# Mixture-of-experts stage: two of four gate/up products as float32r pieces, x copied by ScalarE, gate weight read through the owner's register, loop lap starting with the transposes

## The chip, the cores and the metric

The kernel runs on one core of one Trainium2 chip. The time is device microseconds of one execution; a smaller time is better. The kernel before takes 1219.33 us (median of 3 runs, 1219.15 to 1221.19).

## The reference

The reference is one decoder block on 2048 rows of width 512: a state-space mixer, a cross attention and a mixture of experts, each behind a layer norm and added to its input. The change touches only the last part:

```python
router_logits = (x @ gate_w).astype(jnp.float32)
scores = jax.nn.sigmoid(router_logits)
_, selected = jax.lax.top_k(scores + expert_bias[None, :], K)        # K = 2 of E = 16
top_scores = jnp.take_along_axis(scores, selected, axis=1)
top_scores = top_scores / (top_scores.sum(-1, keepdims=True) + 1e-20)
shared = jax.nn.silu(x @ shared_gate_w) * (x @ shared_up_w) @ shared_down_w
comb = jnp.zeros((T, E), jnp.float32).at[jnp.arange(T)[:, None], selected].add(top_scores)
routed = jnp.zeros_like(x)
for e in range(E):
    gu = x @ experts_gate_up[e]                                      # 512 -> 2 x 256
    g, u = jnp.split(gu, 2, axis=-1)
    routed = routed + comb[:, e:e + 1] * (jax.nn.silu(g) * u @ experts_down[e])
return (shared + routed).reshape(b, s, h)
```

## The kernel before

The mixer and the attention run first (the first 900 us of the span); nothing there is changed. `experts_phase` then sorts the 4096 (row, expert) pairs into 47 tiles of 128 rows, each tile owned by one expert, and works through the tiles, numbered n = 0 to 46. Each of TensorE (PE), VectorE (DVE), ScalarE (ACT), GpSimd (POOL) and the DMA queue of SyncE (SP) has its own program; they meet only at semaphores, and each engine runs its program in the written order.

For a tile n the work is:

- POOL gathers the 128 rows into one of six buffers `xg` (L1512). A row carries its 512 values and behind them its 16 gate weights.
- PE turns them (`transpose_x`, four 128x128 transposes, L1879, semaphore `tx`), and DVE copies the result from PSUM to `xgT` (L1588, `txc`). `xgT` has two buffers.
- PE multiplies by the owner's gate/up weights (`gate_up`, L1909, semaphore `gu`): four float32 products over k. The profile lists each float32 product as two matmuls, so eight matmuls a tile. The weights are read from `ring`, at a slot that is read into a register from the table `own_i`.
- ACT takes the silu of the first half (L1750, `sg`), DVE multiplies by the second half (L1694, `h`), PE turns `h` (`transpose_h`, L1918, `th`); this stands in the middle of the next tile's `gate_up`.
- The product with the down weights is made of float32r pieces: a number is split as high + low, where high is its float32r copy. ACT writes the high pieces (`down_high` from `ring`, L1757; `hT_high`, L1762), DVE the low ones (`down_low`, L1706; `hT_low`, L1712), and PE does high*high, high*low and low*high, six float32r matmuls a tile (`down`, L1927 to L1929, semaphore `dn`).
- ACT scales the result by the row's gate weight `share` (L1771), and POOL adds it into `out` with two indirect DMAs (L1523). `share` is made by DVE: 16 gates times a one-hot `mask`, then a sum (L1699, L1700).

In the steady state PE's order is: `gate_up(n)` with `transpose_h(n-1)` in its middle, `transpose_x(n+1)`, `down(n-1)`. The programs of ACT and DVE are written out for all 47 tiles, and each loads the ring slot of a tile from `own_i` (one value) once per tile, ahead of its read of `ring` (L1428). PE's program is a loop of 7 laps with six tiles each (L1952), with three tiles ahead of it and two behind. At the start of a lap PE loads 12 values (six owners, six slots) into registers with one instruction (L1888). ACT, DVE and PE each have a sequencer, which carries out the register loads and the waits in program order and hands the other instructions to the engine; its own instructions stand in the profile's rows under PEldq, ACTq and DVEq. Expert weights come through a ring of four slots, filled by SP.

Of the kernel before, what the change touches and what calls it, by code (L numbers as in the profile page):

```python
# [11 lines left out]
F32R = mybir.dt.float32r  # L12
# [4 lines left out]
P = 128  # L17
# [1291 lines left out]
def experts_phase(nc, dram, x1, score, ident, out, kept):  # L1309
# [8 lines left out]
    E = 16  # L1318
# [12 lines left out]
    CUTS = 6  # L1331
    HALF = mybir.dt.float16
    ROW = D + E
    xn_rows = dram["xn_rows"]

    with ExitStack() as ctx:
# [38 lines left out]
        source = sb("source", [P, T, TOP, TILES], HALF)  # L1375
        place = sb("place", [P, PAIRS, P], HALF)
        listed = sb("listed", [P, TOP, TILES])
# [4 lines left out]
        mask = sb("mask", [P, TILES, E])  # L1382
        share = sb("share", [P, TILES])
        shares = sb("shares", [P, E])
        logit = sb("logit", [P, P])
# [9 lines left out]
        xg = sb("xg", [P, XG, ROW])  # L1395
        xgT = sb("xgT", [P, 2, KD * P])
        sg = sb("sg", [P, 2, F])
# [22 lines left out]
                 "xTc", "logits", "score", "route_a", "route_mm", "table", "slots", "scattered", "su", "ss", "sh",  # L1420
                 "sd", "sacc", *(f"xg{i}" for i in range(XG)), "tx", "txc", "gu", "sg", "h", "th", "thigh", "tlow", "whigh", "wlow", "dn", "yc",
# [4 lines left out]
        def slot_of(engine, n):  # L1426

            _, (place_of,) = nc.values_load_multi_w_load_instructions(  # L1428
                own_i[0:1, n, 1:2], max_val=RING - 1, min_val=0, engines=[engine],
                skip_runtime_bounds_check_because="the table holds it masked with RING - 1")  # L1430
            return place_of

        def down_weights(place_of):

            return ring[:, bass.ds(place_of, 1), WUP:WUP + KF * D].rearrange("p o c -> p (o c)")

        @block.sync
# [117 lines left out]
        def _(dve):  # L1555
# [28 lines left out]

            def copy_x(n, p):

                dve.wait_ge(s["tx"], n + 1)
                nc.vector.tensor_copy(xgT[:, p, :], ps_x[p][:, :]).then_inc(s["txc"], 1)  # L1588

# [90 lines left out]
            for j in DOWN[0:2]:  # L1680
                add_shared(j)
            copy_x(0, 0)
            for j in DOWN[2:4]:
# [3 lines left out]
                                           op0=ALU.add, op1=ALU.add).then_inc(s["dest"], 1)  # L1687
            V.then(nc.vector.tensor_tensor(mask[:, :, :], iota_e[:, :, :].to_broadcast(jwide),
                                           owner[:, :, :].to_broadcast(jwide), ALU.is_equal))

# [4 lines left out]

            def weigh(n):

                at_least(dve, s["share"], n)
                V.then(nc.vector.tensor_tensor(shares[:, :], xg[:, n % XG, D:ROW], mask[:, n, :], ALU.mult))  # L1699
                nc.vector.tensor_reduce(share[:, n:n + 1], shares[:, :], AX.X, ALU.add).then_inc(s["share"], 1)  # L1700

            def low_weights(n):

                slot_n = slot_of(mybir.EngineType.DVE, n)
                dve.wait_ge(s["whigh"], n + 1)
                nc.vector.tensor_tensor(down_low[:, :], down_weights(slot_n), down_high[:, :], ALU.subtract  # L1706
                                        ).then_inc(s["wlow"], 1)
# [7 lines left out]
            weigh(0)  # L1715
            for n in range(TILES):
                if n + 1 < TILES:
                    copy_x(n + 1, (n + 1) % 2)
                gated(n, n % 2)
                if n + 1 < TILES:  # L1720
                    weigh(n + 1)
                low_weights(n)
                low_h(n, n % 2)

        @block.scalar
        def _(act):
# [25 lines left out]
            def high_weights(n):  # L1752

                slot_n = slot_of(mybir.EngineType.Activation, n)
                act.wait_ge(s["gu"], n + 1)
                at_least(act, s["dn"], n)
                nc.scalar.activation(down_high[:, :], down_weights(slot_n), ACT.Copy).then_inc(s["whigh"], 1)  # L1757

            def high_h(n, p):
                act.wait_ge(s["th"], n + 1)  # L1760
                at_least(act, s["dn"], n)
                nc.scalar.activation(hT_high[:, :], ps_h[p][:, 0:KF * P], ACT.Copy).then_inc(s["thigh"], 1)  # L1762

            def copy_y(n, p):
# [6 lines left out]
                nc.scalar.activation(y[:, n % YB, :], ps_y[p][:, :], ACT.Copy, scale=share[:, n:n + 1]).then_inc(s["yc"], 1)  # L1771

            silu(0, 0)
            act.wait_ge(s["table"], 1)
            high_weights(0)
            for n in range(1, TILES):
                high_h(n - 1, (n - 1) % 2)
                silu(n, n % 2)
                high_weights(n)
                copy_y(n - 1, (n - 1) % 2)  # L1780
# [4 lines left out]
        def _(pe):  # L1785
# [111 lines left out]
            def gate_up(n, p, own, between=None, second=None):  # L1897

                pe.wait_ge(s["wready"], own[0])
                pe.wait_ge(s["txc"], n + 1)  # L1900
                at_least(pe, s["h"], n - 1)
                if isinstance(n, int) and n == 1:
                    pe.wait_ge(s["sacc"], 4)
                for k in range(KD):
                    if between is not None and k == KD // 2:
                        transpose_h(*between)
                    if second is not None and k == KD // 2:
                        transpose_x(*second)
                    ins = nc.tensor.matmul(ps_gu[p][:, :], xgT[:, p, k * P:(k + 1) * P],  # L1909
                                           weights(own)[:, k * 2 * F:(k + 1) * 2 * F],  # L1910
                                           start=(k == 0), stop=(k == KD - 1))
# [27 lines left out]
            def bodies(n, count, first, lap=0, last=False):  # L1939

                own = owners(n, count)
                for m in range(count):
                    more, q = divmod(first + m + 1, XG)
                    body(n + m, (m + 1) % 2, own[m],
                         after=None if last and m == count - 1 else (q, lap + more))

            transpose_x(0, 0, 0, 0)
            pe.wait_ge(s["table"], 1)
            pe.wait_ge(s["sacc"], 1)
            gate_up(0, 0, owners(0, 1)[0], second=(1, 1, 1, 0))  # L1950
            bodies(1, 2, 1)
            with pe.Fori(0, (TILES - 5) // STEP) as i:  # L1952
                bodies(STEP * i + 3, STEP, 3, i)
            bodies(TILES - 2, 2, (TILES - 2) % XG, (TILES - 2) // XG, last=True)
            transpose_h(TILES - 1, 0)
# [95 lines left out]
```

## Time and profile before

| | |
|---|---|
| median of the runs | 1219.33 us |
| the profiled execution, its own time | 1220.97 us |
| its span (first to last instruction) | 1218.0 us |
| PE matmul busy | 1159.5 us (95%) |
| DVE busy | 766.5 us (63%) |
| ACT busy | 519.6 us (43%) |
| POOL busy | 387.6 us (32%) |
| mean granted TensorE clock | 0.994 |
| the tiles of the experts | about 935 to 1212 us |

The busy shares are means over the whole span, and only the last quarter of it is changed, so what counts is the rows of that quarter. Matmuls overlap in the records: one that starts every 0.23 us is listed as 0.39 us long. The distance from start to start is the time that it takes of the engine. A time is given from the start of the span.

### The profile page before, as it was taken

The numbers are of one execution on the slowest core, as the hardware profiler recorded it, in microseconds if no ns is written. First come the engines' busy times: TensorE is split into PE (matmuls) and PEld (weight loads), VectorE is DVE, ScalarE is ACT, GpSimd is POOL, SyncE is SP. The second block draws the span as 40 slices with busy tenths as digits, with TensorE's granted clock in tenths as the row PEclk, the third lists the DMA queues.
The fourth block names the chain that finished last, engine by engine and source line by source line (L and its number), as shares of the span: only waits on it lengthen the run. The fifth ranks groups of instructions, "written<-read, shape, count | busy, mean of one in ns | idle before, by whom it ended". The sixth has DMA issues, their size and how long they took to land. (4 is left out here: it accounts for less than half of the span.)

```text
span 1218.0 us, 31770 instructions
## 1 busy us (share of the span) xinstructions
PE 1159.5 (95%) x13279; PEld 600.5 (49%) x13280; DVE 766.5 (63%) x1244; ACT 519.6 (43%) x716; POOL 387.6 (32%) x502
## 2 busy tenths in 40 slices
PE   6999999999999999999999999999999999999997
PEld 3444434444545544544545554444444555555554
DVE  3743596756788665668575787877657444455443
ACT  3321223533554453545453455555632434444443
POOL 5212311221221230132032221110102477777775
PEclk9999999999999999999999999999999999999998
DMA  8330785104284210355500246300135676788640
GB/s 196 103 88 22 186 174 112 36 16 119 60 158 96 65 33 20 84 123 107 106 25 16 68 100 93 87 3 3 72 105 171 171 181 117 163 231 234 176 89 5
DMA packets 119605, 122.26 MB, mean 100 GB/s; under 512 B 25472, under 2 KB 84992, under 8 KB 119344
## 3 DMA queue, kind: packets, MB, share of 16 engines
q1 hardware_dynamic: 101744, 98.59, 31.7%
q0 software_dynamic: 17008, 21.16, 9.4%
q8 instruction: 99, 1.62, 0.6%
q10 hardware_dynamic: 720, 0.61, 0.2%
q14 instruction: 34, 0.28, 0.1%
HBM read 94.63 MB, written 40.77 MB: 111 GB/s over the span
## 5 line engine op out<-in xcount | busy, mean ns | idle before, releaser
L684 DVE TENSOR_REDUCE mx<-ps_m 128x2 f32<-128x1024 f32 x256 | 312.9, 1222 | 192.8 <-PE ps_m L1025 188.7
L893 ACT ACTIVATE prob<-ps_s 128x1024 f32<-128x1024 f32 x256 | 261.9, 1023 | 322.7 <-PE ps_s L1025 321.8
L1025 PE MATMUL acc<-xnT,wring 128*32 128x512 f32 x1888 | 249.0, 592 | 0.6 <-DVE first_z L620 0.6
L1909 PE MATMUL ps_gu<-ring,xgT 128*128 x376 | 178.7, 598 | 12.0 <-issue 11.1
L1523 POOL DMA_INDIRECT out<-y,dest x92 | 144.7, 1573 | 76.9 <-ACT y L1771 57.7
L1025 PE MATMUL ps_s<-q_stack,k_stack 99*32 99x512 bf16 x2048 | 161.7, 380 | 4.4 <-ACT prob L893 3.8
L1025 PE MATMUL ps_m<-k_stack,q_stack 96*32 96x512 bf16 x1952 | 153.2, 380 | 9.8 <-DVE mx L684 8.2
L1210 PE MATMUL ps_o<-prob,values 128*32 128x128 f32 x4096 | 138.4, 273 | 0.0
L1210 PEld LDWEIGHTS ps_o<-prob,values 128*32 128x32 f32 x4096 | 116.3, 110 | 44.7 <-issue 39.2
L1025 PEld LDWEIGHTS ps_m<-k_stack,q_stack 96*32 96x32 bf16 x1952 | 55.7, 96 | 127.3 <-issue 72.8
L1706 DVE TENSOR_TENSOR down_low<-ring,down_high 128x1024 fp32r<-128x1024 f32 x47 | 57.6, 1226 | 67.1 <-ACT down_high L1757 67.1
L1909 PEld LDWEIGHTS ps_gu<-ring,xgT 128*128 128x128 f32 x376 | 67.3, 191 | 64.0 <-issue 61.0
L1025 PEld LDWEIGHTS ps_s<-q_stack,k_stack 99*32 99x32 bf16 x2048 | 59.0, 96 | 77.6 <-issue 41.5
L1023 PE MATMUL acc<-xnT,wring 128*128 128x512 f32 x184 | 85.6, 603 | 2.1 <-DVE xz L602 2.0
L1025 PEld LDWEIGHTS acc<-xnT,wring 128*32 128x32 f32 x1888 | 65.8, 109 | 43.1 <-issue 6.1
L1757 ACT ACTIVATE down_high<-ring 128x1024 fp32r x47 | 49.6, 1056 | 72.9 <-PE acc L1929 72.6
L1025 PE MATMUL acc<-wring,xz 128*32 128x512 f32 x576 | 76.5, 593 | 0.0
L430 POOL TENSOR_SCALAR mneg<-mx 128x16 f32<-128x16 f32 x32 | 10.1, 317 | 195.7 <-DVE mx L684 195.7
L1588 DVE COPY xgT<-ps_x 128x512 f32<-128x512 f32 x47 | 32.5, 692 | 55.2 <-PE ps_x L1879 55.2
L602 DVE SCALAR_TENSOR_TENSOR xz<-acc,convw,xz 128x511 f32<-128x511 f32 (+2 forms) x84 | 62.7, 746 | 3.9 <-ACT xz L974 1.9
L1512 POOL DMA_INDIRECT xg<-xn_rows,token x47 | 48.4, 1031 | 27.9 <-DVE token L1666 13.9
L1023 PEld LDWEIGHTS acc<-xnT,wring 128*128 128x128 f32 x184 | 34.4, 193 | 41.9 <-issue 32.7
(289 smaller groups left out, 1369.0 us busy)
## 6 DMA issues: line engine op xcount, KB each, us to landing
ring<-in_w_experts SPq DMA_DIRECT2D x96, 256.0 KB, 5.1
wring<-in_w_in SPq DMA_DIRECT2D x80, 256.0 KB, 4.3
q_stack<-part_rows SPq DMA_DIRECT2D x96, 128.0 KB, 4.7
wring<-in_w_out SPq DMA_DIRECT2D x32, 256.0 KB, 2.9
part_rows<-part SPq DMA_DIRECT2D x20, 384.0 KB, 3.8
out<-x SPq DMA_DIRECT2D x4, 1024.0 KB, 4.8
xt<-in_x SPq DMA_DIRECT2D x14, 256.0 KB, 4.6
k_stack<-part_rows SPq DMA_DIRECT2D x48, 64.0 KB, 4.1
```

The costliest lines, as they stand in the source:

```text
L602: ins = nc.vector.scalar_tensor_tensor(out=xz[:, i, tap:], in0=bank(b, 5 + i)[:, :SEQ - tap], scalar=convw[:, i, 3 - tap:4 - tap], in1=xz[ ...
L684: nc.vector.tensor_reduce(mx[:, n % G, 2 * u:2 * u + 2], ps_m[:, :, :], AX.X, ALU.max).then_inc(s_max, 1)
L893: nc.scalar.activation(prob[:, slot % PROB, :, :], ps_s[:, :, :], ACT.Exp, scale=SCALE).then_inc(s_exp, 1)
L1023: return nc.tensor.matmul(dst, stationary, moving, start=start, stop=stop)
L1025: ins = nc.tensor.matmul(dst[c:c + 32, :], stationary[:, c:c + 32], moving, start=start, stop=stop, tile_position=(0, c))
L1210: ins = nc.tensor.matmul(out_rows.rearrange("p (t i) -> p t i", i=VW), values[:, t, g, :], weights[:, a, :, :], start=(t == 0 and r == 0), ...
L1512: pool.indirect_dma_start(out=xg[:, n % XG, :], out_offset=None, in_=xn_rows[:, :], in_offset=bass.IndirectOffsetOnAxis(ap=token[:, n:n + ...
L1523: pool.indirect_dma_start(out=out[:, :], out_offset=bass.IndirectOffsetOnAxis(ap=dest[:, k, n:n + 1], axis=0), in_=y[:, n % YB, :], in_off ...
L1588: nc.vector.tensor_copy(xgT[:, p, :], ps_x[p][:, :]).then_inc(s["txc"], 1)
L1706: nc.vector.tensor_tensor(down_low[:, :], down_weights(slot_n), down_high[:, :], ALU.subtract).then_inc(s["wlow"], 1)
L1757: nc.scalar.activation(down_high[:, :], down_weights(slot_n), ACT.Copy).then_inc(s["whigh"], 1)
L1909: ins = nc.tensor.matmul(ps_gu[p][:, :], xgT[:, p, k * P:(k + 1) * P], weights(own)[:, k * 2 * F:(k + 1) * 2 * F], start=(k == 0), stop=(k ...
```

## The change

1. `gate_up` does the first two of its four products in float32 as before (`WHOLE` = 256 columns of x) and the last two (`SPLIT_K` = 2) from pieces, as `down` does: six float32r matmuls, with `transpose_h` between the two groups. The new pieces are `xgT_high` and `up_high` (written by ACT) and `xgT_low` and `up_low` (written by DVE), with the semaphores `xhigh`, `uhigh`, `xlow`, `ulow`. Each has one buffer. `up_high` and `up_low` lie where `place` was.
2. x is copied out of PSUM by ACT, in two instructions of 256 columns (`high_x`), no longer by DVE in one of 512. `xgT` now has one buffer.
3. `share` is one column read through a register that holds the owner, so `mask` and the two small DVE instructions go. ACT and DVE now load two values (owner and slot) a tile. On ACT the load stands between the silu of a tile and the copy of the next tile's x.
4. In PE's loop a step is now `transpose_x(n+1)`, `down(n-1)`, `gate_up(n+1)` with `transpose_h(n)` in it, so that a lap begins with transposes, and ends with the six float32r matmuls of `gate_up`.

```diff
+    SPLIT_K = 2
+    WHOLE = (KD - SPLIT_K) * P
...
+        def owner_of(engine, n):
+
+            _, (own, place_of) = nc.values_load_multi_w_load_instructions(
+                own_i[0:1, n, :], max_val=E, min_val=0, engines=[engine],
...
+            def low_x(n, p):
+
+                dve.wait_ge(s["xhigh"], n + 1)
+                nc.vector.tensor_tensor(xgT_low[:, :], ps_x[p][:, WHOLE:D], xgT_high[:, :], ALU.subtract
+                                        ).then_inc(s["xlow"], 1)
...
+            def weigh(n, own):
+
+                nc.vector.tensor_copy(share[:, n:n + 1], xg[:, n % XG, D - 1:ROW][:, bass.ds(own, 1)]).then_inc(s["share"], 1)
...
+            def low_up(n, place_of):
+
+                dve.wait_ge(s["uhigh"], n + 1)
+                nc.vector.tensor_tensor(up_low, up_weights(place_of), up_high, ALU.subtract).then_inc(s["ulow"], 1)
...
             for n in range(TILES):
-                if n + 1 < TILES:
-                    copy_x(n + 1, (n + 1) % 2)
                 gated(n, n % 2)
                 if n + 1 < TILES:
-                    weigh(n + 1)
-                low_weights(n)
+                    low_x(n + 1, (n + 1) % 2)
+                    own_next, slot_next = owner_of(mybir.EngineType.DVE, n + 1)
+                    weigh(n + 1, own_next)
+                    low_up(n + 1, slot_next)
+                if n:
+                    low_weights(n, slot_n)
                 low_h(n, n % 2)
...
+            def high_x(n, p):
+
+                act.wait_ge(s["tx"], n + 1)
+                nc.scalar.activation(xgT[:, :], ps_x[p][:, 0:WHOLE], ACT.Copy).then_inc(s["txc"], 1)
+                nc.scalar.activation(xgT_high[:, :], ps_x[p][:, WHOLE:D], ACT.Copy).then_inc(s["xhigh"], 1)
+
+            def high_up(n, place_of):
+
+                at_least(act, s["gu"], n)
+                nc.scalar.activation(up_high, up_weights(place_of), ACT.Copy).then_inc(s["uhigh"], 1)
...
             for n in range(1, TILES):
+                slot_n = slot_next
                 high_h(n - 1, (n - 1) % 2)
                 silu(n, n % 2)
-                high_weights(n)
+                if n + 1 < TILES:
+                    _, slot_next = owner_of(mybir.EngineType.Activation, n + 1)
+                    high_x(n + 1, (n + 1) % 2)
+                    high_up(n + 1, slot_next)
+                high_weights(n, slot_n)
                 copy_y(n - 1, (n - 1) % 2)
...
-                for k in range(KD):
...
+                for k in range(KD - SPLIT_K):
+                    nc.tensor.matmul(ps_gu[p][:, :], xgT[:, k * P:(k + 1) * P],
+                                     weights(own)[:, k * 2 * F:(k + 1) * 2 * F], start=(k == 0), stop=False)
+                if between is not None:
+                    transpose_h(*between)
+                pe.wait_ge(s["xlow"], n + 1)
+                pe.wait_ge(s["ulow"], n + 1)
+                for k in range(SPLIT_K):
+                    rows, cols = slice(k * P, (k + 1) * P), slice(k * 2 * F, (k + 1) * 2 * F)
+                    nc.tensor.matmul(ps_gu[p][:, :], xgT_high[:, rows], up_high[:, cols], start=False, stop=False)
+                    nc.tensor.matmul(ps_gu[p][:, :], xgT_high[:, rows], up_low[:, cols], start=False, stop=False)
+                    ins = nc.tensor.matmul(ps_gu[p][:, :], xgT_low[:, rows], up_high[:, cols], start=False,
+                                           stop=(k == SPLIT_K - 1))
                 ins.then_inc(s["gu"], 1)
...
-            def body(n, p, own, after=None):
-                gate_up(n, p, own, between=(n - 1, 1 - p))
-                if after is not None:
-                    transpose_x(n + 1, 1 - p, *after)
+            def step(n, p, own, q, lap):
+
+                pe.wait_ge(s["wready"], own[0])
+                transpose_x(n + 1, 1 - p, q, lap)
                 down(n - 1, 1 - p)
+                gate_up(n + 1, 1 - p, own, between=(n, p))
```

On ACT, in the written-out part for the tiles, one tile of the kernel before reads as follows (`sg` is the silu, TENSOR_LOAD the load from the table, ISA the register arithmetic ahead of an instruction with an address from a register):

```order
L1750 ACTIVATE sg<-ps_gu 128x256
L1428 TENSOR_LOAD own_i
L1757 ISA
L1757 ACTIVATE down_high<-ring 128x1024
L1771 ACTIVATE y<-acc,share 128x512
L1762 ACTIVATE hT_high<-ps_h 128x256
```

One tile of the changed kernel, on ACT at the same place:

```order
L1773 ACTIVATE sg<-ps_gu 128x256
L1432 TENSOR_LOAD own_i
L1783 ACTIVATE xgT<-ps_x 128x256
L1784 ACTIVATE xgT_high<-ps_x 128x256
L1789 ISA
L1789 ACTIVATE up_pieces<-ring 128x1024
L1778 ISA
L1778 ACTIVATE down_high<-ring 128x1024
L1803 ACTIVATE y<-acc,share 128x512
L1794 ACTIVATE hT_high<-ps_h 128x256
```

Three instructions are new, and all three stand between the load and the copy of the down weights.

On PE, the start of a lap in the kernel before (the last matmuls of `down` ahead of the branch, then the lap's load and the first matmuls of `gate_up`):

```order
L1927 MATMUL acc<-down_high,hT_high 128x512
L1928 MATMUL acc<-down_low,hT_high 128x512
L1929 MATMUL acc<-down_high,hT_low 128x512
L1952 UNCONDITIONAL_BRANCH
L1952 ISA
L1888 TENSOR_LOAD own_i
L1900 REGISTER_ALU
L30 REGISTER_ALU
L1909 ISA
L1909 MATMUL ps_gu<-ring,xgT 128x512
```

And in the changed kernel, from the last matmuls of `gate_up` on:

```order
L1956 MATMUL ps_gu<-up_pieces,xgT_high 128x512
L1957 MATMUL ps_gu<-up_pieces,xgT_high 128x512
L1958 MATMUL ps_gu<-up_pieces,xgT_low 128x512
L2005 UNCONDITIONAL_BRANCH
L2005 ISA
L1932 TENSOR_LOAD own_i
L1920 ISA
L30 REGISTER_ALU
L1923 MATMUL ps_x<-ident,xg 128x128 x4
```

The load of the 12 values still stands right behind the branch; what stands ahead of it is now the part of `gate_up` that waits for `ulow`, and what stands behind it is the transposes of x.

## Rows read from the trace of the kernel before

**Rows 1.** Waits from 937 to 1210 us: who waited, for what, total, times, longest

```profile
PE ps_gu L1909 <- issue: 11.1, 7, 1.9
```

**Rows 2.** Timeline of one tile: start, length, engine, line, instruction, idle before it

```profile
1045.24 0.60 PE L1879 MATMUL ps_x<-ident,xg 128*128 128x128 f32 x4
...
1045.44 0.38 ACT L1750 ACTIVATE sg<-ps_gu 128x256 f32<-128x256 f32 x1 [1.33 <-PE ps_gu L1909]
...
1045.88 0.69 DVE L1588 COPY xgT<-ps_x 128x512 f32<-128x512 f32 x1 [1.17 <-PE ps_x L1879]
...
1047.06 1.88 PE L1909 MATMUL ps_gu<-ring,xgT 128*128 x4
...
1047.41 1.06 ACT L1757 ACTIVATE down_high<-ring 128x1024 fp32r x1 [1.58 <-PE acc L1929]
...
1048.37 0.67 ACT L1771 ACTIVATE y<-acc,share 128x512 f32<-128x512 f32 x1
...
1048.62 1.23 DVE L1706 TENSOR_TENSOR down_low<-ring,down_high 128x1024 fp32r<-128x1024 f32 x1 [1.43 <-ACT down_high L1757]
1048.77 0.38 PE L1918 MATMUL ps_h<-ident,h 128*128 128x128 f32 x2
...
1048.99 1.88 PE L1909 MATMUL ps_gu<-ring,xgT 128*128 x4
...
1050.71 0.60 PE L1879 MATMUL ps_x<-ident,xg 128*128 128x128 f32 x4
```

**Rows 3.** Instructions of L1888, PE's load from the table: prologue, one lap, behind the loop

```profile
L1888 PEldq TENSOR_LOAD <-own_i x2: 730/870/1011, 935.3 to 937.4; - x2
...
L1888 PEldq TENSOR_LOAD <-own_i x1: 2972/2972/2972, 1056.3 to 1056.3; - x1
...
L1888 PEldq TENSOR_LOAD <-own_i x1: 1006/1006/1006, 1194.1 to 1194.1; - x1
```

**Rows 4.** Instructions of L1428, one value on ACT and DVE: ns least/median/most

```profile
L1428 ACTq TENSOR_LOAD <-own_i x47: 272/279/479, 942.7 to 1205.4; - x47
L1428 DVEq TENSOR_LOAD <-own_i x47: 300/304/891, 943.6 to 1205.8; - x47
```

**Rows 5.** A lap's end, 1055 to 1060 us: L1952's branch, then the timeline

```profile
L1952 PEldq COMPARE_BRANCH  x1: 215/215/215, 1055.9 to 1055.9; - x1
...
1055.23 0.42 DVE L1712 TENSOR_TENSOR hT_low<-ps_h,hT_high 128x256 fp32r<-128x256 f32 x1
...
1057.76 0.39 PE L1929 MATMUL acc<-down_high,hT_low 128*128 128x512 f32 x1
...
1059.59 0.69 PE L1909 MATMUL ps_gu<-ring,xgT 128*128 x1 [1.44 <-issue]
```

**Rows 6.** Timeline of the last tile, where PE waited for DVE

```profile
1209.30 0.42 DVE L1712 TENSOR_TENSOR hT_low<-ps_h,hT_high 128x256 fp32r<-128x256 f32 x1
...
1209.82 0.47 PE L1927 MATMUL acc<-down_high,hT_high 128*128 128x512 f32 x1 [2.84 <-DVE down_low L1706]
...
1210.12 0.39 PE L1928 MATMUL acc<-down_low,hT_high 128*128 128x512 f32 x1
```

**Rows 7.** Windows: length, busy of PE, PEld, DVE, ACT, POOL, granted clock, DMA share, GB/s

```profile
937.78:941.20 3.42, 3.42 (x9) 1.76 (x8) 2.27 (x6) 0.00 (x0) 0.96 (x2) 0.50 0.84 268
941.20:1205.20 264.00, 252.94 (x915) 146.06 (x913) 130.54 (x276) 109.79 (x183) 179.61 (x129) 1.00 0.66 161
```

**Rows 8.** Timeline of PE ahead of the first tile

```profile
935.17 0.66 PE L1879 MATMUL ps_x<-ident,xg 128*128 128x128 f32 x4 [0.83 <-DMA xg<-xn_rows,token]
...
936.81 2.84 PE L1909 MATMUL ps_gu<-ring,xgT 128*128 x4 [0.98 <-DVE xgT L1588]
```

**Rows 9.** POOL's costliest groups: line, engine, instruction, count, busy, mean ns, idle before

```profile
L1523 POOL DMA_INDIRECT out<-y,dest x92 | 144.7, 1573 | 76.9 <-ACT y L1771 57.7
...
L1512 POOL DMA_INDIRECT xg<-xn_rows,token x47 | 48.4, 1031 | 27.9 <-DVE token L1666 13.9
```

More of the change, by code:

```diff
@@ L1424, in experts_phase, with up_weights @@
         block = ctx.enter_context(nc.Block())
[L1426 to L1431, printed above, removed]
+        def owner_of(engine, n):
+            _, (own, place_of) = nc.values_load_multi_w_load_instructions(
+                own_i[0:1, n, :], max_val=E, min_val=0, engines=[engine],
+                skip_runtime_bounds_check_because="the tables are clamped: an owner is at most E - 1, a slot is "
+                                                  "masked with RING - 1")
+            return own, nc.s_assert_within(place_of, 0, RING - 1, skip_runtime_bounds_check_because=(
+                "the table holds it masked with RING - 1"))
+        def up_weights(place_of):
+            return ring[:, bass.ds(place_of, 1), (KD - SPLIT_K) * 2 * F:WUP].rearrange("p o c -> p (o c)")
         def down_weights(place_of):
             return ring[:, bass.ds(place_of, 1), WUP:WUP + KF * D].rearrange("p o c -> p (o c)")
+        first_down = ring[:, 0, WUP:WUP + KF * D]
+        first_up = ring[:, 0, (KD - SPLIT_K) * 2 * F:WUP]
         @block.sync
@@ L1771, in copy_y @@
                 nc.scalar.activation(y[:, n % YB, :], ps_y[p][:, :], ACT.Copy, scale=share[:, n:n + 1]).then_inc(s["yc"], 1)
+            act.wait_ge(s["wready"], 1)
+            act.wait_ge(s["inverse"], 1)
+            nc.scalar.activation(up_high, first_up, ACT.Copy).then_inc(s["uhigh"], 1)
+            high_x(0, 0)
+            nc.scalar.activation(down_high[:, :], first_down, ACT.Copy).then_inc(s["whigh"], 1)
+            act.wait_ge(s["table"], 1)
+            _, slot_next = owner_of(mybir.EngineType.Activation, 1)
             silu(0, 0)
-            act.wait_ge(s["table"], 1)
-            high_weights(0)
+            high_x(1, 1)
+            high_up(1, slot_next)
             for n in range(1, TILES):
+                slot_n = slot_next
                 high_h(n - 1, (n - 1) % 2)
                 silu(n, n % 2)
-                high_weights(n)
+                if n + 1 < TILES:
[3 more added lines that the diff above has]
+                high_weights(n, slot_n)
                 copy_y(n - 1, (n - 1) % 2)
@@ L1895, in weights, with gate_up @@
                 return ring[:, bass.ds(own[1], 1), :].rearrange("p o c -> p (o c)")
-            def gate_up(n, p, own, between=None, second=None):
-                pe.wait_ge(s["wready"], own[0])
+            def gate_up(n, p, own, between=None):
                 pe.wait_ge(s["txc"], n + 1)
@@ L1931, in down, with steps @@
                 ins.then_inc(s["dn"], 1)
-            def body(n, p, own, after=None):
-                gate_up(n, p, own, between=(n - 1, 1 - p))
-                if after is not None:
-                    transpose_x(n + 1, 1 - p, *after)
+            def step(n, p, own, q, lap):
+                pe.wait_ge(s["wready"], own[0])
+                transpose_x(n + 1, 1 - p, q, lap)
                 down(n - 1, 1 - p)
-            def bodies(n, count, first, lap=0, last=False):
-                own = owners(n, count)
+                gate_up(n + 1, 1 - p, own, between=(n, p))
+            def steps(n, count, first, lap=0):
+                own = owners(n + 1, count)
                 for m in range(count):
                     more, q = divmod(first + m + 1, XG)
-                    body(n + m, (m + 1) % 2, own[m],
-                         after=None if last and m == count - 1 else (q, lap + more))
+                    step(n + m, (first + m) % 2, own[m], q, lap + more)
             transpose_x(0, 0, 0, 0)
@@ L1949, in _ @@
             pe.wait_ge(s["sacc"], 1)
-            gate_up(0, 0, owners(0, 1)[0], second=(1, 1, 1, 0))
-            bodies(1, 2, 1)
+            own = owners(0, 2)
+            pe.wait_ge(s["wready"], own[0][0])
+            gate_up(0, 0, own[0])
+            pe.wait_ge(s["wready"], own[1][0])
+            transpose_x(1, 1, 1, 0)
+            gate_up(1, 1, own[1], between=(0, 0))
+            steps(1, 2, 1)
             with pe.Fori(0, (TILES - 5) // STEP) as i:
-                bodies(STEP * i + 3, STEP, 3, i)
-            bodies(TILES - 2, 2, (TILES - 2) % XG, (TILES - 2) // XG, last=True)
+                steps(STEP * i + 3, STEP, 3, i)
+            steps(TILES - 2, 1, (TILES - 2) % XG, (TILES - 2) // XG)
+            down(TILES - 2, 1)
             transpose_h(TILES - 1, 0)
```

47 lines of the change are left out of this document (18 added, 29 removed).

## The prediction

> **What bounds the kernel now.** I read the waits of the experts' stage first: PE, the busiest engine, has only one wait that comes back, seven times before L1909, 11.1 us in all [rows 1]. The windows say the same: PE is busy 252.9 of 264 us, at the full clock [rows 7]. So between the laps of its loop PE never waits, and a tile costs what PE has to do. The timeline of one tile gives it from start to start [rows 2]: transposes of x at 1045.24 and again at 1050.71, so 5.47 us a tile. Half of `gate_up` (four matmuls) is 1050.71 - 48.99 = 1.72, two transposes 48.99 - 48.77 = 0.22, four of them 0.44, and `down` is the rest from 1045.24 to 47.06, 1.82 - 0.44 = 1.38, which is 0.23 a float32r matmul. Sum: 1.72 + 0.22 + 1.72 + 0.44 + 1.38 = 5.48.
>
> The seven waits are the starts of the laps. The last row of `down` starts at 1057.76 and would let the next matmul start at 57.99; it starts at 1059.59 [rows 5]: 1.60 us lost (listed as 1.44, since a matmul's record runs on for 0.16). In this time PE's sequencer loads 12 values in 2.97 us [rows 3]. It reached the branch at 1055.9, just behind the end of `hT_low`, 1055.23 + 0.42 = 1055.65, for which the last wait ahead of the branch asks [rows 5]. So a lap start costs 1059.59 - 1055.65 = 3.94 us from the last wait that comes true, less the PE work that is handed over behind it: 57.99 - 55.65 = 2.34.
>
> **PE's work.** Two float32 products (1.72) become six float32r matmuls (1.38): -0.34 a tile, so 5.13. If nothing else changed, 47 x 0.34 = 16.
>
> **The new chain of a tile.** The last six matmuls of `gate_up(n+1)` now wait for `ulow`, which hangs on `gate_up(n)` by way of ACT and DVE. I count from the moment G at which PE could start the next thing behind `gate_up(n)` (1045.24) [rows 2]:
> - silu starts at G + 0.20 (1045.44), 0.38 long.
> - Then ACT loads from the table, ahead of the copy of x. One value takes 0.28 on ACT, 0.30 on DVE [rows 4]. For two there is no row of ACT. PE's loads are 1.006 for 4 values and 2.97 for 12 [rows 3], 0.245 a value, and this line gives 0.27 for one, what ACT shows; so two take 0.52. Bounds: 0.28 (the second is free) and 0.73 (PE's two values, the first load of the stage [rows 3]). The load starts with the silu, since the sequencer stood before its wait. The first `high_x` so starts at 0.20 + 0.52 + 0.08 for handing over = 0.80. Its other condition, the transposes, is true at 0.64 (DVE's copy started at 1045.88).
> - `high_x` twice, each 128x256 from PSUM as the silu (0.38); ACT's instructions overlap by 0.10 (1047.41 + 1.06 against 48.37) [rows 2]: starts at 0.80, 1.09, `high_up` at 1.38. It is as large as `down_high`: 1.06, end 2.44.
> - `low_up` starts 0.15 later, as `down_low` did (48.62 against 48.47), and takes 1.23: end 3.82. DVE's own side (`low_x` at 1.5, load of two values 0.57, `share`) is done by 2.4 and is covered by `high_up`; if the load took 0.9 it would no longer be.
> - PE: after such a wait the first matmul starts 0.10 behind the end on DVE and the second 0.30 later [rows 6]. Then 0.30 + 0.10 + 5 x 0.23 = 1.55 from the end of `low_up`: the next G is at 5.36.
>
> PE's own work is 5.13, so PE waits 0.23 in each tile, in front of the float32r matmuls. I take 5.35: -0.12 a tile where the change's arithmetic promised -0.34. `down(n)` isn't late: `up_high` gone, `down_high` ends at 3.40, `down_low` at 4.95, `hT_low` at 5.3, and PE asks for it at 5.35 + 0.44. In the first tile of a lap silu and load are done before the transposes come, so its copy starts at 0.64 and the tile takes 5.19.
>
> **The lap start.** The load of 12 values is not changed (2.97), and neither is the rest of the 3.94. But the last wait ahead of the branch is now `ulow`, and behind it only 1.55 us of PE work is handed over, no longer 2.34. The gap grows from 1.60 to 2.40, +0.80 in each of 7 laps = +5.6. The transposes at its head don't shorten it, since they too stand behind the load.
>
> The 45 tiles from the second `gate_up` to the last: 7 x (5.19 - 5.47) = -2.0, 38 x (5.35 - 5.47) = -4.6, laps +5.6: together -1.0.
>
> **The clock.** In the stage TensorE ran at the lower level (0.50, 1.2 GHz) once, for 3.4 us from 937.8 [rows 7], after idle times of 0.83 and 0.98 us in the 2.6 us before [rows 8]. After the lap gaps, listed at up to 1.9, it stayed at 2.4 GHz [rows 1, 7]. The new gap would be listed as 2.40 - 0.16 = 2.24, longer than any that it stood and longer than the two that it did not. I expect the fall behind most laps, and take 5 of 7, by no more than that 1.8 in two pieces sufficed once and 1.9 in one did not. Such a stretch halves 3.4 us of PE work, 1.7 lost, of which 5.19 - 5.13 = 0.06 hides: 1.6 each, 5 x 1.6 = +8.0 (bounds 0 and 7 x 1.7 = 11.9).
>
> The Trainium skill (TensorE: Matmul & The Clock Gate, "HAM oscillation — how this bites in real kernels") warns only of PE idle gaps longer than this one. By it the clock would stay up and this term be 0. The rows of the fall at 937.8 speak against it.
>
> **Prologue, end, other queues.** Ahead of the first tile ACT's copy of x is shorter (256 columns), but `gate_up(0)` waits for `low_up(0)` and `low_x(0)` behind four additions on DVE, and tile 1 waits for its copy; on the other side the low stretch of 937.8 may go. By the same lengths I get between -0.7 and +0.7, and take 0. At the end `down(45)` to `down(46)` wait as before: 0. POOL has 2 x 1.57 + 1.03 = 4.2 us a tile [rows 9] and pauses of 0.3, 5.1 in all, less than 5.35: it stays hidden. The mask (once) and the two small DVE instructions of a tile save nothing, since DVE had idle time there.
>
> The Trainium skill (DMA: Bandwidth & Descriptors, "Latency and other measured facts") gives a table load a floor of about 600 ns; the rows here show 279 for one value [rows 4]. By the page two values would take at least 0.6, the tile 5.43, and the sum would be 38 x 0.08 = 3 us higher.
>
> **Sum.** -1.0 + 8.0 = +7.0. The profiled execution took 1220.97 (span 1218.0, 3.0 around it), 1.6 above the median 1219.33; I add to both: span 1225, median 1226.3.
>
> **Rivals.**
> - The clock stays up (or falls once): 1218.3 to 1220. For it: it stood gaps of 1.9. Chance 0.18, about no change.
> - Faster: the second value costs ACT nothing, or the load is over before the silu ends. Then the copy starts at 0.64, each tile takes 5.19, 45 x 0.28 = -12.6, laps +5.6: -7.0, so 1212.3 with the clock up. If moreover the lap gap stays at 1.60, because the sequencer gets less to do behind the load than I think, the clock stays up too and it is 1206.7. Against it: loads of PE grow with their values. Chance 0.17. It decides the sign from a tile of about 5.3 on, if the clock stays up.
> - Slower still: the two-value load is at its upper bound of 0.73 (or DVE's comes to lie on the chain), the tile takes 5.56: 38 x 0.21 = +8 on top, 1234 with the falls of the clock. Chance 0.07.
> - POOL binds instead (5.1 a tile at least, laps apart): it would only cap the faster case, by nothing that changes its sign.
> - My forecast, 3 to 7 falls of the clock, 1222 to 1231: chance 0.58.
>
> **Numbers.** Two medians of this kernel that differ by less than about 0.2% (2.4 us) can't be told apart. The range 1215 to 1230.5 takes in the clock case, the upper part of the faster one and most of mine. Of mine all but a little is slower by over 0.2%; of the clock case three quarters are within: faster 0.18, same 0.16, slower 0.66.
>
> **What would show it.** In the profile after: a tile of 5.35 from start to start of the transposes; an idle time before L1956 that ends with DVE L1720, 0.2 us in most tiles; TENSOR_LOAD of 0.5 us on ACT between silu and L1783; seven PE gaps of 2.2 to 2.7 before L1923 by issue; granted clock under 1 in the stage behind most laps. I am wrong if ACT's load stays near 0.28, if the gaps before L1923 are under 1.9, or if the clock stays at 1.00 after gaps of over 2.

## The result and the profile after

The changed kernel takes 1213.21 us (median of 4 runs, 1209.61 to 1213.75), the kernel before beside it 1220.26 (4 runs, 1219.15 to 1221.47): a ratio of 0.9936, 95% interval 0.9913 to 0.9958. It is faster by 0.6%, where I had forecast 1226.3 and slower. The profiled execution of the changed kernel is its fastest: 1209.61 us, span 1207.6, mean granted clock 0.999 (the others 0.995 to 0.996).

Its page, busy time and the scatter of POOL:

```profile
PE 1150.4 (95%) x13372; PEld 616.1 (51%) x13374; DVE 804.0 (67%) x1243; ACT 588.4 (49%) x857; POOL 409.2 (34%) x502
...
L1536 POOL DMA_INDIRECT out<-y,dest x92 | 165.3, 1797 | 47.6 <-issue 28.3
```

Its loads from the table: PE's in the seven laps, then those of ACT and DVE over the stage (ns least/median/most):

```profile
L1932 PEldq TENSOR_LOAD <-own_i x7: 847/850/857, 952.1 to 1154.5; - x7
```

```profile
L1432 ACTq TENSOR_LOAD <-own_i x46: 484/578/1312, 933.1 to 1190.0; - x46
L1432 DVEq TENSOR_LOAD <-own_i x46: 524/536/1325, 938.3 to 1191.2; - x46
```

The load of 12 values, 2.97 us long before [rows 3], takes 0.85, though it asks for as many values. That is where the gain is: of PE's seven lap gaps (1.60 us worked out for one of them [rows 1, 5]) nothing is left among the waits. Two views show it. The first is the timeline at a lap start, where the load began at 1053.9: the last matmul of `gate_up` starts at 1054.67 and would let the next go at 1054.90, and the lap's first transpose starts 0.19 later. The second is the waits of the stage, where PE's only wait that comes back is the new one for `low_up`:

```profile
1054.67 0.40 PE L1958 MATMUL ps_gu<-up_pieces,xgT_low 128*128 128x512 f32 x1
...
1055.09 0.65 PE L1923 MATMUL ps_x<-ident,xg 128*128 128x128 f32 x4
```

```profile
POOL out L1536 <- issue: 28.3, 84, 0.7
...
PE ps_gu L1956 <- DVE up_pieces L1720: 7.8, 24, 0.5
```

The starts of the transposes divide the time of both profiled executions:

| stretch | before | after | difference |
|---|---|---|---|
| tile 0 to tile 2 | 10.94 | 9.81 | -1.1 |
| tile 2 to tile 46 (44 tiles, 7 laps) | 253.62 | 247.55 | -6.1 |
| tile 46 to the end | 18.26 | 17.83 | -0.4 |

(Before: 935.18, 946.12, 1199.74, 1218.0; after: 932.41, 942.22, 1189.77, 1207.6. The 2.8 us by which the stage begins earlier lie in work that isn't changed; the stage itself is 7.6 shorter, close to the 7.0 between the medians.) The middle stretch hides two terms of opposite sign. Before, a lap's first tile lasts 7.31 on average (7.10 to 7.61) and the others 5.47, so the laps hold 7 x 1.84 = 12.9 us, which go. So its tiles became longer by 6.8 in all: 5.63 us on average, where they took 5.47. This is the second surprise. I had worked out 5.35, and some tiles do take 5.34 to 5.38, but most don't. One that doesn't, start, length, engine, instruction (its ACT load comes first, from the list of loads):

```profile
L1432 ACTq TENSOR_LOAD <-own_i x1: 714/714/714, 1104.9 to 1104.9; - x1
```

```profile
1104.65 0.60 PE L1923 MATMUL ps_x<-ident,xg 128*128 128x128 f32 x4
...
1104.77 1.55 POOL L1536 DMA_INDIRECT out<-y,dest  x1 [0.31 <-DMA out<-y,dest]
1104.85 0.38 ACT L1773 ACTIVATE sg<-ps_gu 128x256 f32<-128x256 f32 x1 [1.22 <-PE ps_gu L1958]
1105.01 0.48 PE L1975 MATMUL acc<-down_high,hT_high 128*128 128x512 f32 x1
...
1105.62 0.38 ACT L1783 ACTIVATE xgT<-ps_x 128x256 f32<-128x256 f32 x1 [0.38 <-PE ps_x L1923]
...
1106.16 1.06 ACT L1789 ACTIVATE up_pieces<-ring 128x1024 fp32r x1
...
1106.47 1.88 PE L1948 MATMUL ps_gu<-ring,xgT 128*128 x4
...
1107.38 1.23 DVE L1720 TENSOR_TENSOR up_pieces<-ring,up_pieces 128x1024 fp32r<-128x1024 f32 x1 [0.24 <-ACT up_pieces L1789]
...
1107.95 2.10 POOL L1536 DMA_INDIRECT out<-y,dest  x1 [0.30 <-issue]
...
1108.52 1.22 DVE L1714 TENSOR_TENSOR down_low<-ring,down_high 128x1024 fp32r<-128x1024 f32 x1
...
1108.75 0.47 PE L1956 MATMUL ps_gu<-up_pieces,xgT_high 128*128 128x512 f32 x1 [0.18 <-DVE up_pieces L1720]
...
1110.24 0.60 PE L1923 MATMUL ps_x<-ident,xg 128*128 128x128 f32 x4
```

The order of events is the one predicted, and each step has nearly the length predicted (silu at +0.20, from the first copy to `low_up` 1.76 for 1.79, `low_up` 1.23), but for one: the load that starts with the silu takes 0.71 us, 0.22 more than the 0.49 that the same load takes elsewhere, and the tile takes 5.59, 0.24 more than 5.35. From tile 13 on (counted by the transposes that start it), 23 of 34 of ACT's loads are over 0.55, up to 1.31. All but one of those begin 0.05 to 0.09 us behind the start of a scatter of POOL (here 1104.77 against 1104.86; the one left starts 0.28 ahead of a scatter); those that begin 0.9 or more into one take 0.49. In tiles 3 to 11 ACT's loads stand 0.7 or more into a scatter and take 0.49; there it is DVE's loads that take 1.0 to 1.3, beside POOL's gather, and the tiles take 5.6 to 5.9. A gather beside it isn't enough for that: in tiles 40 to 42 DVE's loads begin 0.01 to 0.3 into one as well and take 0.53.

### The profile page after: what moved, and what is told of

Its sections match the earlier page's. It is cut to its first block and busy times, and to the rows that moved or that the text cites. A ratio compares the mean times of both kernels' runs of the same rounds, so it can differ in the third digit from the quotient of the medians.

```text
span 1207.6 us, 32147 instructions
## 1 busy us (share of the span) xinstructions
PE 1150.4 (95%) x13372; PEld 616.1 (51%) x13374; DVE 804.0 (67%) x1243; ACT 588.4 (49%) x857; POOL 409.2 (34%) x502
## 5 line engine op out<-in xcount | busy, mean ns | idle before, releaser
L1536 POOL DMA_INDIRECT out<-y,dest x92 | 165.3, 1797 | 47.6 <-issue 28.3
L1948 PE MATMUL ps_gu<-ring,xgT 128*128 x188 | 88.9, 595 | 1.3 <-ACT xgT L1783 1.2
L1720 DVE TENSOR_TENSOR up_pieces<-ring,up_pieces 128x1024 fp32r<-128x1024 f32 x46 | 56.4, 1227 | 7.6 <-ACT up_pieces L1789 7.2
L416 POOL COPY values<-keys 128x64 f32<-128x64 f32 x32 | 9.1, 299 | 142.2 <-PE ps_o L1210 142.2
L420 POOL CAST part<-rest 128x512 bf16<-128x512 f32 x20 | 13.4, 668 | 124.0 <-DVE rest L677 124.0
```

The source lines that it names most:

```text
L1536: pool.indirect_dma_start(out=out[:, :], out_offset=bass.IndirectOffsetOnAxis(ap=dest[:, k, n:n + 1], axis=0), in_=y[:, n % YB, :], in_off ...
L1720: nc.vector.tensor_tensor(up_low, up_weights(place_of), up_high, ALU.subtract).then_inc(s["ulow"], 1)
L1948: nc.tensor.matmul(ps_gu[p][:, :], xgT[:, k * P:(k + 1) * P], weights(own)[:, k * 2 * F:(k + 1) * 2 * F], start=(k == 0), stop=False)
```

## The experiments

Three questions are open: why the load of 12 values is fast, whether the clock would have fallen had it stayed slow, and what draws out the other loads. The expectations name the theories by letters and say what each expects. The kernels of the experiments mask an owner with 31 ahead of PE's wait for its weights, one more register operation a tile. The first run shows what this costs, and the change itself once more.

**e0: the changed kernel with that register operation.**

```diff
-                return [(own[2 * m], in_ring(own[2 * m + 1])) for m in range(count)]
+                return [(own[2 * m] & 31, in_ring(own[2 * m + 1])) for m in range(count)]
```

> The changed kernel with one register operation more on PE in each tile (owner & 31 ahead of the wait for wready), as all kernels here have it. All theories: as the changed kernel, 1213 us within 1.5; PE's load of 12 values 0.85 us, no gap at a lap's start.

1211.93 us (1210.05 to 1213.0) against 1219.01 of the kernel before: 0.9935 (0.9918 to 0.9952), as the change itself. The operation costs nothing that shows, and the load of 12 values again takes 0.85.

**Where the table is read.** A tile has two values, 8 bytes, and a lap starts at tile 3, 9, 15 and so on. Before, PE loaded the owners from the lap's first tile on; the new `step` multiplies by the next tile's weights, so it reads from one tile further on:

```diff
-                own = owners(n, count)
+                own = owners(n + 1, count)
```

The 12 values so begin at byte 24 + 48i of the table before, which is 8 past a multiple of 16, and at 32 + 48i after, a multiple of 16. (Bytes are counted from the start of the table; where the table itself lies in SBUF isn't on record.) One theory (A) is that this alone decides how long the load takes. The test is to shift the whole table by one tile in each kernel, and by two in the kernel before.

**e1: the kernel before, the table shifted by 8 bytes.**

```diff
-        own_i = sb("own_i", [1, TILES, 2], mybir.dt.int32)
+        own_i = sb("own_i", [1, 1 + TILES, 2], mybir.dt.int32)
...
-                    own_i[0:1, bass.ds(n, count), :].rearrange("p g w -> p (g w)"), max_val=E, **one_engine)
+                    own_i[0:1, bass.ds(n + 1, count), :].rearrange("p g w -> p (g w)"), max_val=E, **one_engine)
```

> The kernel before with the table own_i shifted by one tile (8 bytes), so that a lap's load of 12 values starts at byte 32 + 48 i and no longer at 24 + 48 i; nothing else changed but the & 31. Theory A (a load is fast where it starts on a multiple of 16 bytes: four values at once): the load takes 0.85 us, its 3.94 us become 1.8, less than the 2.34 us of PE work handed over, so the seven gaps (11.1 us) go and the time is about 1220.3 - 12 = 1208. Rival B (the load is fast in the changed kernel because float32r matmuls run beside it, or because it stands at another place of the lap): it stays at 2.97 us and the time at 1220.

1206.58 us (1203.33 to 1206.77): 0.9896 (0.9878 to 0.9913), 12.4 us under the kernel before and 5.3 under the changed one of e0. PE's loads of the laps, and a window inside the stage (length, busy of PE, PEld, DVE, ACT, POOL, granted clock, DMA share, GB/s):

```profile
L1888 PEldq TENSOR_LOAD <-own_i x7: 846/849/862, 947.8 to 1145.0; - x7
```

```profile
950.00:1178.00 228.00, 228.00 (x833) 132.87 (x832) 117.84 (x248) 100.44 (x168) 172.87 (x124) 1.00 0.70 169
```

The load falls from 2.97 to 0.85 with nothing else changed but the register operation of e0, the lap gaps are gone, and PE has no idle time in the window (the kernel before: 216.94 of the same 228). From tile 3 on every tile takes 5.47 to 5.49.

**e2: the changed kernel, the table shifted by 8 bytes** (the same edit on its lines).

> The changed kernel with the same shift of the table by 8 bytes: a lap's load starts at byte 40 + 48 i. Theory A: it takes 2.97 us again, each of the seven laps starts with a gap before the transposes of 2.2 us or a little more, the clock falls behind some of them, and the time is 1213 plus 10 to 20: 1223 to 1233 (this is my forecast of the changed kernel with tiles that are 0.28 us longer). Rival B: load 0.85, 1213.

1234.23 us (1232.36 to 1236.16): 1.0119 (1.0102 to 1.0137), 22.3 over e0. The load, a lap start, and one of the low stretches that follow:

```profile
L1932 PEldq TENSOR_LOAD <-own_i x7: 2980/3177/3419, 954.3 to 1176.6; - x7
```

```profile
1031.24 0.39 PE L1958 MATMUL ps_gu<-up_pieces,xgT_low 128*128 128x512 f32 x1
...
1034.00 1.04 PE L1923 MATMUL ps_x<-ident,xg 128*128 128x128 f32 x4 [2.37 <-issue]
1034.69 0.78 PE L1975 MATMUL acc<-down_high,hT_high 128*128 128x512 f32 x1
```

```profile
1034.11:1037.52 3.41, 3.41 (x11) 2.83 (x12) 1.26 (x3) 1.60 (x3) 1.93 (x2) 0.50 0.72 135
```

This is the kernel that I had predicted without knowing it: gaps listed at 1.94 to 2.69, median 2.46 (worked out 2.24), and, behind 5 of the 7 laps, a stretch at 0.50, that is 1.2 GHz (959.0, 996.6, 1034.1, 1071.7, 1180.9). The tile that follows takes 6.70 to 6.88 there. So both the lap term and the clock term had about the right size for a load of 3 us, the lap term a little small: a lap's first tile takes 8.24 on average here, by my sum 5.19 + 2.40 = 7.59.

**e5: the kernel before, the table shifted by 16 bytes.** The edit of e1 with 2 in place of 1. It tells A from the rival that any shift, or any other layout of the memory, would do.

> The kernel before with the table shifted by two tiles (16 bytes): a lap's load starts at byte 40 + 48 i, again 8 behind a multiple of 16. Theory A (the multiple of 16 bytes decides): load 2.9 to 3.3 us, seven gaps, 1219. Rival (any shift, or the longer table, makes it fast): load 0.85, 1207.

1221.41 us (1219.82 to 1222.62): 1.0018 (1.0007 to 1.0029) against 1219.39; the load is slow as before (six of the seven are listed, the first took 3.56) and PE's gaps are there as before:

```profile
L1888 PEldq TENSOR_LOAD <-own_i x6: 2921/2964/3334, 985.0 to 1158.8; - x6
```

```profile
PE ps_gu L1909 <- issue: 11.6, 7, 2.0
```

A shift by 8 bytes turns fast into slow and slow into fast; one by 16 leaves the slow load slow (it wasn't tried on the fast one). The place of the first value decides, and A stands, for the two places that were tried: at a multiple of 16 and 8 past one.

**e3: ACT's load ahead of the silu.** In the changed kernel, so that it is carried out while ACT waits for `gate_up` (theory C1: the load on ACT is what makes the tile long).

```diff
                 high_h(n - 1, (n - 1) % 2)
-                silu(n, n % 2)
                 if n + 1 < TILES:
                     _, slot_next = owner_of(mybir.EngineType.Activation, n + 1)
+                silu(n, n % 2)
+                if n + 1 < TILES:
                     high_x(n + 1, (n + 1) % 2)
```

> The changed kernel with ACT's load alone moved ahead of the silu's wait; DVE's stays between low_x and share. The tile after both moves was 5.25 us, after none 5.63. Theory C1 (ACT's load, 0.5 to 1.3 us, is what lengthens the tile from the 10th on, DVE's, 1.0 to 1.3 us, that of the tiles 3 to 10): tiles 3 to 10 stay at 5.6 to 5.8, the rest at 5.25 to 5.3, time 1198 to 1202. Rival C2 (as soon as ACT's load is gone, DVE's meets POOL's DMA instructions in all tiles): tiles of 5.5 and more throughout, 1206 to 1210.

1202.4 us (1199.51 to 1203.72): 0.9862 (0.9844 to 0.988), against 0.9935 with the load in its old place. Most tiles now take 5.24 to 5.27, but those from 4 to 9 still 5.75 to 5.9, and 10 and 11 take 5.5 to 5.6. There the other load, DVE's, takes 1.0 to 1.4 and stands on the chain ahead of `low_up`:

```profile
L1432 ACTq TENSOR_LOAD <-own_i x46: 483/492/686, 933.2 to 1178.7; - x46
L1432 DVEq TENSOR_LOAD <-own_i x46: 527/732/1415, 938.3 to 1181.3; - x46
```

Away from the start of a scatter ACT's loads take 0.49 (median), as C1 has it. The rival C2 was right in its first half only: from tile 22 on most of DVE's loads now begin beside the start of a scatter and take 0.6 to 1.1, but most tiles stay near 5.25: there a longer load on DVE is hidden.

**e4: both loads early.** ACT's as in e3, and DVE's ahead of its wait for the silu:

```diff
             for n in range(TILES):
+                if n + 1 < TILES:
+                    own_next, slot_next = owner_of(mybir.EngineType.DVE, n + 1)
                 gated(n, n % 2)
                 if n + 1 < TILES:
                     low_x(n + 1, (n + 1) % 2)
-                    own_next, slot_next = owner_of(mybir.EngineType.DVE, n + 1)
                     weigh(n + 1, own_next)
```

> The changed kernel with ACT's load of a tile ahead of the silu's wait (where ACT is idle) and DVE's ahead of the wait for the silu. Theory C (the loads of two values on the chain from one gate_up to the next make the tile 5.63 us instead of 5.19, since they take 0.5 to 1.3 us): tiles of about 5.2 us, 45 x 0.4 = 18 us less, 1195 to 1200. Rival D (POOL is what sets 5.6 us: one of its two scatters lasts 2.1 us instead of 1.57 beside the two long DVE subtractions, sum 4.7 us and pauses of 0.9): tiles stay at 5.5 or more, 1209 to 1213.

1197.14 us (1195.03 to 1199.45): 0.9818 (0.98 to 0.9837), 14.8 under e0. Tiles take 5.24 to 5.26 (the one at a lap's start 0.28 more), and PE hardly rests. All scatters are still there, so POOL (the rival D) isn't what set the 5.6 us. The window of e1, and PE's last float32r group of a tile with the transposes behind it:

```profile
950.00:1178.00 228.00, 227.38 (x952) 154.65 (x950) 155.16 (x258) 167.88 (x302) 186.59 (x127) 1.00 0.70 171
```

```profile
1054.44 0.47 PE L1958 MATMUL ps_gu<-up_pieces,xgT_high 128*128 128x512 f32 x1
1054.75 0.40 PE L1959 MATMUL ps_gu<-up_pieces,xgT_high 128*128 128x512 f32 x1
...
1055.93 0.60 PE L1925 MATMUL ps_x<-ident,xg 128*128 128x128 f32 x4
```

The group costs 55.93 - 54.44 = 1.49 without any wait: its first matmul takes 0.31, the others 0.23 or 0.24.

**e6: the scatters left out.** Does POOL draw out the loads (theory E), or the weights' DMAs and the other engines? In the changed kernel, loads where they were, POOL only raises the semaphore of each scatter, so the experts' share of the output is left out; the gathers stay.

```diff
-                pool.indirect_dma_start(
-                    out=out[:, :], out_offset=bass.IndirectOffsetOnAxis(ap=dest[:, k, n:n + 1], axis=0),
-                    in_=y[:, n % YB, :], in_offset=None, bounds_check=TOKENS - 1, oob_is_err=False,
-                    compute_op=ALU.add).then_inc(done, 16)
+                pool.sem_inc(done, 16)
```

> The changed kernel (with the & 31) without POOL's two scatters a tile: only the semaphores are raised, so the experts' part of the output is left out. Theory E (ACT's and DVE's loads are drawn out by POOL's indirect DMA instructions that run beside them): all of ACT's loads 0.49 to 0.50 us, DVE's 0.53 but for those beside a gather, tiles of 5.35 us, which is what I worked out, 45 x 0.28 = 12 us less: 1196 to 1201. Rival F (the loads are drawn out by the weights' DMAs or by other engines' reads): loads still spread up to 1.3 us, time above 1206.

1201.45 us (1200.24 to 1203.76): 0.9852 (0.9832 to 0.9871). Its loads:

```profile
L1432 ACTq TENSOR_LOAD <-own_i x46: 482/493/687, 937.9 to 1184.5; - x46
L1432 DVEq TENSOR_LOAD <-own_i x46: 523/529/771, 943.0 to 1185.7; - x46
```

Tile after tile takes 5.36, the length worked out for loads that nothing draws out, and the first of a lap some 0.3 more. All engines still load and the weights still come, so neither is enough to draw out a load; with the scatters gone it doesn't happen. The run takes away the instruction on POOL and the transfers that it starts at once (the DMA share from 950 to 1170 falls from 0.71 to 0.45) and doesn't tell which of the two does it. It doesn't clear the gathers either, since none of the loads in its tiles lies beside one. The leftover between 5.36 here and 5.25 in e4 is what the undisturbed load costs on ACT's path.

**e8, e9 and e10: both loads early, and the lap begins with `gate_up` again.** The last 0.28 at a lap start might go if the float32 matmuls, which wait for less, stood first. e8 and e9 are one kernel: both loads early, a lap's read that stays at a multiple of 16, 16 values a lap; its new lines are below. e10 is e4 again, beside e9 on the same chip.

```diff
-            def step(n, p, own, q, lap):
-
-                pe.wait_ge(s["wready"], own[0])
-                transpose_x(n + 1, 1 - p, q, lap)
+            def body(n, p, own, coming=None, after=None):
+                gate_up(n, p, own, between=(n - 1, 1 - p))
+                if after is not None:
+                    pe.wait_ge(s["wready"], coming[0])
+                    transpose_x(n + 1, 1 - p, *after)
                 down(n - 1, 1 - p)
-                gate_up(n + 1, 1 - p, own, between=(n, p))
```

> Both loads early, and PE's lap begins with gate_up and ends with down, as in the kernel before; a lap loads 16 values (eight tiles, so that the wait for the next tile's weights stands ahead of its transposes) from a multiple of 16 bytes. The load should take 4 x 0.28 = 1.1 us; with the rest 0.97 that is 2.1 us, less than the 2.34 us of PE work handed over behind the last wait: no gap, where the lap of the kernel with both loads early still lost 0.28 us each, 2.0 in all: 1195. Rival: the 16-value load is not four times the price of four (or the instruction behind needs more), gaps of 0.3 or more remain: 1197 or above.

> The kernel with both loads early and a lap that begins with gate_up, once more, since its first profiled execution ran with TensorE at the lower clock throughout. By the working given with it: load of 16 values 1.1 us, no gap at the laps' starts, 0.28 x 7 = 2.0 us less than the next kernel of this call. Its times so far (1198.4 against 1197.1 on two chips) speak for the rival, that the laps or the tiles still lose as much elsewhere.

> The kernel with both loads early, whose laps begin with the transposes, on the same chip: 1197, tiles of 5.25 us and 0.28 us more at each lap's start.

e8: 1197.91 us (median of five, 1195.08 to 1199.41), 0.982 (0.98 to 0.984); rows are read from the profile of e9. e9: 1197.02 (1196.75 to 1198.26), 0.9814 (0.9797 to 0.9831). e10: 1197.02 (1196.79 to 1199.14), 0.9814 (0.9796 to 0.9832). The two are equal. In e9 most lap starts do cost only 0.07 to 0.08 (0.28 in e10), and tile 2 to tile 46 takes 231.45 us against 232.99. But its way from tile 0 to tile 1 takes 6.60 against 4.53. The shift of the table puts PE's first load, of 4 values, at byte 8, where it takes 1.19 instead of 0.53; the first `gate_up` starts 1.67 behind the transposes instead of 1.32, and then the granted clock is 0.50 for 3.4 us from 935.6, so that the way from there to the next transposes takes 4.93 instead of 3.21. (A load of 8 values behind it, at a multiple of 16, takes 2.67 while one of DVE's takes 2.80, with gathers but no scatter under way; PE has work handed over the while, and the next tile takes 5.25.) A load of 16 values in a lap takes 1.11:

```profile
L1934 PEldq TENSOR_LOAD <-own_i x7: 1105/1106/1238, 951.1 to 1140.7; - x7
```

The best version stays e4: 1.8% under the kernel before, against 0.6% of the change as made.

## Why the prediction was wrong

**The step that failed** is "The load of 12 values is not changed (2.97)". I took the number of values as what sets the price of a load (0.245 a value, from PE's rows of 4 and 12) and didn't see that the read had moved by one tile, from a place between two multiples of 16 bytes onto one. The rows held a hint that I read past: a slope drawn through PE's own two rows, both of them badly placed. With the load at 0.85 the lap term is not +5.6 but -12.9 + 7 x 0.19 = -11.6, and the gap that was to bring down the clock doesn't exist, so +8.0 becomes 0: the profile after shows 1.00 throughout the stage. The sum would be 1226.3 - 5.6 - 11.6 - 8.0 = 1201.1. (That the laps held 12.9 and not 7 x 1.60 = 11.2 is a size that was off: I took one lap for all, and its gap was among the shorter.) The measured 1213.2 lies near the 1212.3 of my faster rival, but by chance: that rival had the second value cost nothing and the laps grow by 5.6, and neither happened.

**The second error** goes the other way: measured is 1213.2, 12 us more than that. "POOL ... stays hidden" was true of its own time and wrong in its effect. With its scatters the chain's loads are longer, by up to 0.8 us on ACT, and the tile takes 5.63 on average instead of 5.35: over 44 tiles, less 7 x 0.19 of lap starts, 11 us. e6 gives the same by difference, 0.9852 against e0's 0.9935, 0.8% or 10 us. My bound of 0.73 for the load of two values, taken from PE's row, was too low an upper bound; the rows of before have such a load in them (DVE's 0.891 for one value [rows 4]), and it was left aside since DVE's side was covered. The slower rival, to which I gave a chance of 0.07, had a tile of 5.56, and that is near what came.

**What held.** The undisturbed load of two values: 0.49 (0.52 worked out). The chain step by step, and with it 5.36 a tile in e6. The lap gap for a slow load (listed at 2.46 in the median, 2.24 worked out), and the clock: 5 of 7 laps, and about 1.45 us each (6.8 against 5.35; 1.6 worked out). The share of laps was a guess that happened to fit, and its ground was weaker than I took it: I argued from the fall at 937.8 after idle times of 0.83 and 0.98 [rows 7, 8], but at the same place e1 has 0.76 and 0.98 and e2 0.84 and 1.02, and there the clock stayed up. With the load slow again the kernel takes 1234.2, over my 1226.3 by 8. In e2's profile two things are longer than in my sum: the tiles outside the lap starts and the low stretches, 5.61 on average for 5.35 from the first lap on (8 us), and the laps' first tiles, 8.24 for 7.59 (4.6 us). The rule of the Trainium skill that I weighed there (TensorE: Matmul & The Clock Gate, "HAM oscillation — how this bites in real kernels"), which warns only of longer idle gaps, would have left the clock up; the stretches at 0.50 behind gaps of 1.94 to 2.69 us in e2 decide against it. The floor of about 600 ns that the Trainium skill gives for a table load (DMA: Bandwidth & Descriptors, "Latency and other measured facts") doesn't hold here either: 0.49 for two values.

**A size that was off.** PE's work of a tile is 5.25, not 5.13 (e4). The first float32r matmul behind float32 ones takes 0.31 and the group 1.49, where I had 1.38 from a split of 1.82 that gave the transposes 0.44; they take 0.36. So of the 0.34 that the change was to save on PE, 0.22 was to be had, and with the load on ACT's path 0.11.

**The parts of the change by themselves.** Set against e1, where the table is read at a good place and the change's own parts are absent, the changed kernel is slower by 5.3 us. What made it faster than the kernel before is a side effect of the new order of the loop, which moved the read by 8 bytes; the arithmetic in float32r pays (1206.6 to 1197.1) only once the two loads are off the chain.

## What to carry to other kernels

A load from a table into registers has a price of its own that, for four values and more, depends on where its first value lies: lay the table out so that a loop's reads begin at the good place (here a multiple of 16 bytes from its start), and look at the load's row rather than at its count of values. Place a register load ahead of a wait that the engine has anyway, never between a wait and the instruction on which another engine hangs, above all where GpSimd starts indirect DMAs at the same moment. And when one edit changes the order of a loop, list every operand whose index moved with it.

## What the runs showed of the hardware

- PE's register loads from SBUF, by place of the first value in the table. At a multiple of 16 bytes: 0.34 to 0.40 us for 4 values, 0.85 for 12, 1.11 for 16. At 8 bytes past one: 1.00 to 1.02 for 4, 2.9 to 3.6 for 12. The first load of the stage is longer: 0.53 for 4 values at byte 0, 1.19 at byte 8. Other places were not tried, nor what in the sequencer makes it so.
- Two values take the same at either place: 0.49 on ACT, 0.53 on DVE, 0.54 to 0.56 on PE (the last load, byte 368 in the changed kernel, 376 in e2). That is more than four values at the good place (0.35). Whether ACT and DVE would be faster with four was not tried.
- A register load that begins just behind the start of an indirect scatter took up to 1.31 us instead of 0.49 on ACT, and some beside a gather 1.0 to 1.4 instead of 0.53 on DVE; without the scatters none in the tiles did (e6). Seven of ACT's loads that began at the same moment took 0.49 to 0.51 all the same; what spares them is open. For some tiles the length comes back from run to run: at tiles 13, 28 and 39 it is 0.84, 0.93 and 1.07 in the changed kernel, 0.82, 0.91 and 1.05 in e0, 0.82, 0.92 and 1.03 in e2.
- The scatter itself is longer where DVE's work is denser: 1.57 us on average before [rows 9], 1.80 after. In the tile above, the one that lies beside two subtractions of 128x1024 out of SBUF back to back takes 2.10, the one ahead of it 1.55. That DVE is the cause is read from this coincidence alone; no run takes the subtractions away.
- The granted clock fell behind five of seven PE gaps (e2), and behind none of those of up to 1.9 of the kernel before [rows 1, 7]. The length of the gap doesn't order them: it fell behind the one listed at 1.94 in e2, not behind those of 2.61 and 2.40, nor behind one of 1.96 in e5. Nor do the two idle times ahead of the first `gate_up`, 0.76 to 0.87 and 0.98 to 1.02: behind them it fell to 0.50 for 3.4 us in the kernel before, e5 and e9, and not in e1 and e2. What else decides is open.
